# Graph layers on one core: neighbour products begun source by source in pass 0, transposes one tile later in pass 2, an early Ln

## The reference

```
h = relu(layernorm(x));  x = x + sage(relu(sage(h)))           # block 0: two layers
h = relu(layernorm(x));  x = x + expmap0(self + mean(logmap0(h)[src]) @ W)   # block 1
h = relu(layernorm(x));  x = x + three mean layers             # block 2
h = relu(layernorm(x));  x = x + attention over the edges      # block 3
agg = segment_sum(x[src], dst);  agg / max(count, 1)           # what every layer needs
```

## Time and profile before

| what | us |
|---|---|
| median of 3 runs | 2705.43 |
| lowest, highest run | 2700.43, 2722.41 |
| the profiled execution | 2701.79 |
| its span in the profile | 2699.3 |
| PE busy in the span | 1760.8 (65%) |
| DVE, ACT, POOL busy | 1418.9, 1042.0, 1025.5 |

### The profile page before, as it was taken

One profiled execution on the slowest core, in us unless ns is written; L12 is line 12 of the kernel. 1 busy time (PEld: TensorE's weight loads), 2 busy tenths in 40 slices (PEclk: granted clock), 3 DMA queues, 4 the chain that ended last, 5 costly groups with the idle time before them and its releaser, 6 DMA issues.

```text
span 2699.3 us, 48165 instructions
## 1 busy us (share of the span) xinstructions
PE 1760.8 (65%) x10229; PEld 1109.4 (41%) x10229; DVE 1418.9 (53%) x4461; ACT 1042.0 (39%) x3014; POOL 1025.5 (38%) x1355
## 2 busy tenths in 40 slices
PE   2666665699899999989355555645554555555554
PEld 0111111355555565656244444534344444444443
DVE  8888887433656533346244444534344444444444
ACT  3888886432554322212123223323223222233233
POOL 2000001322544310111455555565555655655552
PEclk9999999999999999999566666666666666666766
DMA  1000000100111101013433333333333333333331
GB/s 65 0 0 0 0 0 20 43 26 29 50 51 53 50 27 32 29 60 102 141 96 109 110 96 107 110 104 106 95 103 112 109 94 102 107 100 108 109 94 45
DMA packets 148866, 188.65 MB, mean 70 GB/s; under 512 B 25795, under 2 KB 117316, under 8 KB 148804
## 3 DMA queue, kind: packets, MB, share of 16 engines
q0 software_dynamic: 38784, 105.96, 13.5%
q1 hardware_dynamic: 110020, 82.00, 9.5%
HBM read 162.82 MB, written 25.04 MB: 70 GB/s over the span
## 4 chain that ended last, share of the span: by engine, by line
another core or an unknown queue 20%; DVE 13%; issue 10%; PE 7%; ACT 1%; DVEq 0%; DMA 0%; ACTq 0%
DVE counts L1460 4%; DVE a_score L1463 3%; PE aq_bank L1335 3%; PE acc_bank L1354 3%; DVE counts L1468 1%; DVE a_clipped L1473 1%; DVE counts L1392 1%; PE ap_bank L1341 0%; PE ac_bank L1370 0%; PE ac_bank L1371 0%; DVE counts L1416 0%; DVE a_stat L1424 0%; ACT counts L1300 0%; DVE a_stat L1423 0%
## 5 line engine op out<-in xcount | busy, mean ns | idle before, releaser
L1265 POOL DMA_INDIRECT counts<-keys_values,a_index x808 | 783.3, 969 | 576.9 <-ACT a_index L1280 340.6
L776 PE MATMUL z_bank<-y_parts,counts 128*128 128x384 bf16 (+1 forms) x3750 | 665.7, 329 | 4.1 <-DMA y_parts<-in_L_gnn_bq 4.1
L1335 PE MATMUL aq_bank<-counts 128*128 128x128 bf16 x2424 | 291.9, 263 | 356.6 <-issue 340.5
L1460 DVE TENSOR_TENSOR counts<-aq_bank,counts 128x512 f32<-128x512 f32 x202 | 139.3, 690 | 720.8 <-remote 602.5
L1354 PE MATMUL acc_bank<-counts 128*128 128x136 f32 x1616 | 338.9, 366 | 215.7 <-DVE counts L1468 107.9
L776 PEld LDWEIGHTS z_bank<-y_parts,counts 128*128 (+1 forms) x3750 | 370.0, 99 | 238.6 <-issue 14.1
L1296 ACT ACTIVATE counts<-a_clipped 128x32 f32<-128x32 f32 x202 | 46.1, 228 | 919.2 <-DVE a_clipped L1473 774.8
L1354 PEld LDWEIGHTS acc_bank<-counts 128*128 128x128 f32 x1616 | 288.5, 257 | 255.6 <-DVE counts L1468 129.6
L1335 PEld LDWEIGHTS aq_bank<-counts 128*128 128x128 bf16 x2424 | 211.6, 119 | 416.6 <-issue 406.3
L496 PE MATMUL share_build<-right_build,left_build 128*128 128x300 bf16 x816 | 276.9, 443 | 128.5 <-DVE right_build L434 98.0
L462 ACT ACTIVATE square_build<-iota_b_build,low_build 128x128 bf16<-128x128 bf16 x682 | 237.9, 387 | 2.2
(11 more groups left out here) (153 smaller groups left out, 1871.1 us busy)
## 6 DMA issues: line engine op xcount, KB each, us to landing
counts<-group_rel_rows SPq DMA_DIRECT2D x34, 768.0 KB
counts<-keys_values,a_index POOLq DMA_INDIRECT x808
self_term<-s_out SPq DMA_DIRECT2D x150, 64.0 KB, 1.6
s_in<-self_term SPq DMA_DIRECT2D x150, 64.0 KB, 1.8
residual<-x_in SPq DMA_DIRECT2D x75, 64.0 KB, 1.6
counts<-query_parts SPq DMA_DIRECT2D x34, 96.0 KB
x_in<-in_x SPq DMA_DIRECT2D x50, 64.0 KB, 1.8
x_in<-residual SPq DMA_DIRECT2D x50, 64.0 KB, 1.8
```

Of the source, the lines that this page charges most:

```text
L776: yield s, nc.tensor.matmul(bank(p, dt)[:, 0:width], counts[:, bass.ds(dt.value(P) + s * NA, P)], y3[(p - 1) % 2][:, s, 0:width], start=s ...
L1265: nc.gpsimd.indirect_dma_start(rows_kv[:, j, c, :], None, v.kv, bass.IndirectOffsetOnAxis(index[:, j, c:c + 1], 0)).then_inc(gathered[j], 16)
L1335: ins = nc.tensor.matmul(q_bank[s.slot()][:, c * P:c * P + P], spread[:, g.slot(), (j * GC + c) * P:(j * GC + c) * P + P], queries[:, g.sl ...
L1460: nc.vector.tensor_tensor(prod[:, :].rearrange("p (c d) -> p c d", c=GC), q_bank[s.slot()][:, :].rearrange("p (c d) -> p c d", c=GC), rows ...
```

## The change

Three edits, all in `dense_layers`.

1. In pass 0, PE now issues in each step from dt = 4 on, behind T and P, the z products of one source for all four first tiles of pass 1 (`source_for_first_tiles`, source dt-4). Behind the last step it issues sources 23 and 24 for the four tiles (`finish_first_pass`). `begin` is no longer used between pass 0 and pass 1, and the first four steps of pass 1 hold only T and P.
2. `TURNED[2]` goes from 3 to 4: in pass 2, T, P and ACT's `turned` work on a tile one step later; ACT's `second` goes along, from lag 3 to 4. DVE's `second` and POOL's `self_term` keep their lag 4.
3. One `Ln` of a constant is issued on ACT ahead of pass 0.

```diff
-FILL = {0: (4, 3, 6), 1: (20, 4, 8), 2: (16, 4, 14), 3: (12, 4, 16), 4: (10, 4, 8), 5: (10, 4, 8)}
-TURNED = {0: 2, 1: 1, 2: 3, 3: 2, 4: 1, 5: 1, 6: 2}
+FILL = {1: (20, 4, 8), 2: (16, 4, 14), 3: (12, 4, 16), 4: (10, 4, 8), 5: (10, 4, 8)}
+TURNED = {0: 2, 1: 1, 2: 4, 3: 2, 4: 1, 5: 1, 6: 2}
...
+            def source_for_first_tiles(d):
+                (d + 1).count(pe, y_ready)
+                for n in range(AHEAD):
+                    nc.tensor.matmul(z_bank[n][:, 0:YW + 1], counts[:, bass.ds(d.value(NA) + n * P, P)],
+                                     y3[0][:, bass.ds(d.value(), 1), 0:YW + 1].rearrange("p a d -> p (a d)"),
+                                     start=d.k is None and d.c == 0, stop=False)
...
+            def finish_first_pass(first):
+                for source in range(first, NT):
+                    pe.wait_ge(y_ready, source + 1)
+                    for n in range(AHEAD):
+                        ins = product(1, Num(n), source)
+                        if source == NT - 1:
+                            ins.then_inc(z_ready, 1)
...
+                if begun and p == 1:
+                    stage(lambda d: transpose(p, d), dt, TURNED[p])
+                    stage(lambda d: products(p, d), dt, TURNED[p])
+                    return
...
+                    if p == 0 and not by_edge:
+                        stage(source_for_first_tiles, dt, PEELED - 1)
-                if p and not by_edge:
+                if p == 1 and not by_edge:
+                    finish_first_pass(NT + TURNED[0] - PEELED + 1)
+                if p > 1 and not by_edge:
                     begin(p, AHEAD * EARLY)
...
+            if 0 in passes and not by_edge:
+                chain.step(nc.scalar.activation(stat[:, 0, LOG1:LOG1 + 1], one[:, :], ACT.Ln))
...
-                    stage(lambda d: second(p, d), dt, last)
+                    stage(lambda d: second(p, d), dt, max(last, TURNED[p]) if p < 6 else last)
...
-                over_tiles(chain, step, LAG[p][3] + 2 * (p == 6))
+                over_tiles(chain, step, LAG[p][3] + 2 * (p == 6) + (p == 2))
```

More of the change, by code:

```diff
@@ L770, in bank, with product @@
                 return z_bank[nth(S_IN, p, dt).slot(AHEAD)]
-            def products_of(p, dt, sources):
+            def product(p, dt, source):
                 width = YW + 1 if p == 1 else YW
-                for s in sources:
-                    yield s, nc.tensor.matmul(bank(p, dt)[:, 0:width], counts[:, bass.ds(dt.value(P) + s * NA, P)],
-                                              y3[(p - 1) % 2][:, s, 0:width], start=s == 0, stop=s == NT - 1)
+                return nc.tensor.matmul(bank(p, dt)[:, 0:width], counts[:, bass.ds(dt.value(P) + source * NA, P)],
+                                        y3[(p - 1) % 2][:, source, 0:width], start=source == 0, stop=source == NT - 1)
+            def source_for_first_tiles(d):
[4 more added lines that the diff above has]
+                                     start=d.k is None and d.c == 0, stop=False)
             begun_products = [0] * (PASSES + 1)
@@ L787, in begin @@
                         pe.wait_ge(y_ready, NT * (p - 1) + EARLY)
-                    for _ in products_of(p, Num(n), (source,)):
-                        begun_products[p] = i + 1
+                    product(p, Num(n), source)
+                    begun_products[p] = i + 1
+            def finish_first_pass(first):
[5 more added lines that the diff above has]
+                            ins.then_inc(z_ready, 1)
             def neighbour_sum(p, dt):
@@ L806, in neighbour_sum @@
                 first = EARLY if begun else 0
-                for n in range(first, NT):
+                for source in range(first, NT):
                     if begun and dt.c == 0:
[L809 to L813, removed]
+                        pe.wait_ge(y_ready, NT * (p - 1) + source + 1)
+                    ins = product(p, dt, source)
+                    if source == NT - 1:
+                        ins.then_inc(z_ready, 1)
+                    if source == max(first, TURN_AT[p][0]):
                         stage(lambda d: transpose(p, d), dt, TURNED[p])
-                    if n == max(first + 4, TURN_AT[p][1]):
+                    if source == max(first + 4, TURN_AT[p][1]):
                         stage(lambda d: products(p, d), dt, TURNED[p])
@@ L826, in step @@
                         return
-                    filling = dt.k is None and NT <= dt.c and p < 6 and not by_edge
+                    filling = dt.k is None and NT <= dt.c and 0 < p < 6 and not by_edge
                     if filling and dt.c == NT:
```

## The result

The changed kernel takes 2723.81 us (median of 20 runs, 2705.98 to 2737.79), the kernel before 2707.47 us (20 runs, 2689.51 to 2722.41). The ratio is 1.0064, 95% interval 1.0043 to 1.0085: 16 us slower. The forecast had 2728, and a chance of 0.59 for a change within 1%. The profiled execution took 2724.13 us with a span of 2721.5.

The account below looks back on a forecast made before the run. PE was taken to bound pass 2 (busy 98.36 of 100 us) and to have room in pass 0. Edit 1's -12.1 and pass 2's +36.8 made +24.7 on 2701.8: 2726.5, median put at 2728, range 2703 to 2750.

Parts of the forecast that it names:

- the two rings: Pass 2, waits closing once a step: through POOL's queue, 6.6 us; through next_h waiting for T of tile n-2, 5.6 us.
- its first term: Pass 0, P of tile 2 to P of tile 24: three laps of 3.09 and 19 of 2.15 us, gain 3.0.
- The transition: Last P of pass 0 to first T of pass 1: 15.5 us before, 6.4 after, gain 9.1.
- Pass 0 at the low clock: Rival: pass 0 stays at 1.2 GHz, 18.0 us more, about 2746; chance 0.16.
- Only the shorter ring: Rival: in pass 2 only next_h's wait for T binds, 22 laps at 5.6 us, about 2706; chance 0.13.
- No ring: Rival: in pass 2 no wait loop closes, PE keeps 4.9 us a lap, about 2690; chance 0.12.
- Clock falling in pass 2: Rival: idle PE drops to 1.2 GHz; if in half the laps, some 15 us more, about 2743; chance 0.07.
- the first ring: Pass 2, each step: self_term waits for ys, holding up h_norm, then DVE, ACT and PE; laps of 6.6 us.

Follow-up runs that it names:

- the ring experiments: Changed kernel with POOL's self_term last, with next_h's wait for T moved, with both; and both without edit 2: 2385.92, 2407.95, 2372.21, 2373.97 us.
- experiment with unread products: Kernel before, plus four z products nobody reads behind P in each of steps 4 to 24 of pass 0: 2379.94 us, ratio 0.9975.
- `self_term` last: Changed kernel, in whose pass 2 POOL does self_term last in its step, behind h_norm and the roots: 2385.92 us, ratio 0.9994.
- both rings opened by hand: Changed kernel with POOL's self_term last in pass 2 and the wait for T moved from next_h to log_map: 2372.21 us, ratio 0.9942.
- wait moved: Changed kernel, in whose pass 2 the wait for T of two tiles before stands ahead of log_map, not next_h: 2407.95 us in one run.

## Why the prediction was right

| term | predicted | measured in the profiled run |
|---|---|---|
| pass 0, P of tile 2 to P of tile 24 | -3.0 | 53.08 to 44.18: -8.9 |
| last P of pass 0 to first T of pass 1 | -9.1 | 15.53 to 6.57: -9.0 |
| pass 1 | 0 | 126.72 to 126.21: -0.5 |
| last P of pass 1 to first P of pass 2, with the Ln | +1.4 | 23.41 to 25.27: +1.9 |
| first P to last P of pass 2 | +37.8 | 117.34 to 151.47: +34.1 |
| last P of pass 2 to first T of pass 3 | -2.4 | 12.94 to 10.62: -2.3 |
| sum | +24.7 | +15.4 at the first T of pass 3, +16.4 at the last T of pass 6 |

**Edit 2** was right in its mechanism, and the ring experiments show it rather than argue it: each of the two rings sits where its edges were added up, 6.3 to 6.8 us against 6.6, and 5.54 to 5.71 against 5.6. Which of them is the longer came out as said. The 3.7 us too much are small. Behind the first lap, which took the 7.1 us predicted, twenty laps from P to P are 6.51 on average and not 6.6: 1.9 us (POOL starts L718 0.04 us before L725 ends by the records, and ACT is 0.14 quicker from L955 to L878). The last three laps take 5.81, 4.83 and 3.59, together 14.2, where the sum had 16.0. PE waits 1.44 to 1.85 us for `hT` per step in the loop, 1.6 on average, against 1.7.

**Edit 1** was right in sign and place, but its first term was too small by a factor of three. The term that was mis-sized is the run of laps in pass 0, and two steps of it: that the lap at 2.4 GHz lies near the upper end of 1.70 to 2.33 us, taken as 2.15, and that the clock rises after three laps. The price of a lap at the low clock was right (3.09 us predicted; 3.09 to 3.17 in the run that stayed at the low clock for five). But the laps at 2.4 GHz are mostly 1.83, with about every fourth at 2.0 to 2.4, and 1.95 on average: over 19 laps that is 3.9 of the 5.9 us missed. DVE is busy 28.26 of 40 us, 1.38 of each such lap and not the 1.63 counted from before, and that its instructions wait for one another did not keep the lap from 1.83. The other 2.1 us are the clock, which was up one lap after the first z products and not three. That is the usual case here: of the ten traces with z products in pass 0, eight have the rise between 468.3 and 469.6, one at 474.4 (after three laps, as predicted) and one at 480.6, and that last one ended pass 0 4 us later. The busy time by stretch, after:

```profile
466.00:506.00 40.00, 30.81 (x144) 17.05 (x142) 28.26 (x118) 26.70 (x81) 25.08 (x58) 1.00 0.22 65
```

The transition (6.4 against 6.57 us) was right to 0.2 us. The experiment with unread products shows what pass 0 gained from. That a busier pass 0 raises the clock, which the Trainium skill (TensorE: Matmul & The Clock Gate, Part 1) led one to expect, the trace agrees with: 1.22 us for P in the one kernel and 0.70 in the other.

**Edit 3** gave its 1.28 us, the load's own duration. By the Trainium skill (ScalarE: Activation LUTs, What ACT_TABLE_LOAD costs) it should have given 2.66; the trace and the run with the Ln alone disagree: the stretch from the last T of pass 1 to the first T of pass 2 takes 1.27 and 1.28 us less (22.67 to 21.40 and 21.39).

**The rivals.** Pass 0 at the low clock: out, the clock rose early in all ten traces with z products there. Only the shorter ring: out, the laps are 6.3 to 6.8 us and L718 follows L725 at once; with `self_term` last it is the one that stands. No ring: out, and with both rings opened by hand it gives 2372 us, the time of the kernel without edit 2 (2370 to 2371). Clock falling in pass 2: not in the first profile of the changed kernel, but it happens. In three of the four traces with the first ring closed (changed kernel on the other chip, edit 2 alone, wait moved) the record has the clock low for some 3 us in pass 2, once in two of them and twice in the third. It costs little there. With the wait moved, around the fall at 757.1:

```profile
756.38 0.70 PE L764 MATMUL d_bank<-weights,hT 128*128 128x256 f32 x2 [1.90 <-ACT hT L878]
756.91 5.25 PE L775 MATMUL z_bank<-y_parts,counts 128*128 128x384 bf16 x21
...
762.90 0.70 PE L764 MATMUL d_bank<-weights,hT 128*128 128x256 f32 x2
```

The 21 z products took 5.25 us where others take 3.58, but the next P did not wait for `hT` at all, where its neighbours wait 1.5 to 1.9 us, and it came 6.52 us behind the last one, as this lap does in every turn of the loop. The slack that the ring leaves PE took the loss up. Near the end of pass 2 a fall made a lap some 0.5 us longer (5.26 against 4.83 in the changed kernel, 6.33 against 5.81 with edit 2 alone). So the rival's 15 us don't come: they needed the clock low through half of all laps, 8.0 us of z products in each, and the record has one or two stretches of some 3 us in a pass of about 150.

That 2728 is only 4 us from the 2724 measured is in part luck. The sum of terms was +24.7, and the change is +16.3 between the medians: 8.4 too much. Of these, 2.1 dropped out since the sum was set against the profiled execution and the median then put at 2728, and 2.0 since the kernel before has its median at 2707.5 over 20 runs and not at 2705.4. Neither of the two has to do with the mechanism.

## What to carry to other kernels

When a stage is moved one step later, list every stage on other engines that keeps its step and reads what it writes, and what stands behind that stage in its queue. If the next step needs one of those, a ring closes; add its edges and hold the sum against the lap. Here one instruction of 0.46 us in the wrong place of POOL's queue cost 20 us of pass 2, and a wait two tiles back 14 more. In pass 0 here, where PE stood at the low clock with gaps in each lap, work moved into the gaps paid twice: it was gone elsewhere (9 us), and the clock rose under the chain that sets the lap (8 us). Whether it does so in another stage has to be measured there.

## What the runs showed of the hardware

- Added work made a stage quicker: 84 unread products in pass 0 took 7.7 us off it, P going from 1.22 to 0.70 us.
- With the same z products in pass 0 the clock rose at 468.3 to 469.6 in eight of ten traces, at 474.4 in one and at 480.6 in one.
- A raised clock did not last by itself: up at 455.5 after products from 451.5 on, it was down at 462.3, PE's only work since 457.6 being two T and two P.
- A ring that leaves PE idle takes up a short fall of the clock: 21 z products took 5.25 us instead of 3.58, and the lap stayed at 6.52.
- The opening of pass 3 takes 8.9 to 11.0 us and that of pass 6 6.3 or 8.2, with the same code, by how long the clock stays low. Kernels that differ only hundreds of us ahead differ in that; the parts of this change, measured alone, add up to the whole only within 6 us.
- Between two chips the dense passes agree within 1.2 us in 850, while the attention of the changed kernel takes 1412 us on the one and 1089 on the other (last T of pass 6 to the end of the span).
